# Attention scores of single heads as 32-row products, with unpadded keys and four larger buffers

## The chip, the cores and the metric

The kernel runs on one core of a Trainium2 chip. The metric is device time in microseconds (us), the median of the runs; lower is better. The profile is that of one execution, and its times count from the start of its span.

## The reference, cut to what matters

The input x is 8 batches of 512 tokens by 128 features. A macaron layer is computed in 32-bit floats:

```
x = x + 0.5 * moe(layernorm(x))       # 8 experts, hidden 512, all are applied and summed
x = x + attention(layernorm(x))       # 16 heads of 8 dimensions, causal
x = x + 0.5 * moe(layernorm(x))

moe:       acc += (silu(x @ wg[e]) * (x @ wu[e])) @ wd[e]   for the 8 experts
attention: q, k = rotary(q), rotary(k);  q = q / sqrt(8)
           scores = q @ k.T + q @ rel[clip(j - i, -32, 32)].T    (causal)
           attn = softmax(scores);  ctx = attn @ v + attn @ rel[...];  out = ctx @ wo.T
```

## The kernel before

**The expert passes.** A pass applies all eight experts to one batch. There are 16 passes (8 before the attention, called A, and 8 behind it, called B), each with 32 units of 128 hidden features. A unit is nine products on TensorE, each of 128 stationary columns and 512 moving ones: three for gate (L794, L795, L798), three for up (L730 to L732), two for down and one for down_lo (L813, L814, L821). Three products stand for one, because each operand is split in a high and a low part in the format fp32r. Between them ScalarE makes tanh (L942) and the high part hid_hi (L948), VectorE two products (L1073, L1079) and GpSimd the low part hid_lo (L1247). HB counts the buffers of hid, HH those of hid_hi and hid_lo.

**The attention.** It runs among the units of the passes, batch by batch. The 16 heads of a batch are worked in four groups of four (HG groups, the four places of a group are HQ). There are 32 groups in all (8 batches by 4). A group has four query tiles i = 0 to 3 of 128 queries, and tile i sees the first 128 (i + 1) keys. Its scores are made in 11 tasks, since a bank of PSUM holds 512 columns: one task of four heads for i = 0 (4 x 128 columns), two of two heads for i = 1 (2 x 256), four of one head for i = 2 (384 columns) and four of one head for i = 3 (512 columns). Each task is one product at L876.

A head has 8 dimensions, and q and k have two parts each, so the four part-by-part products of a head take 32 rows of the array. In the tile qq the rows of the four heads of a group are interleaved, every fourth row belonging to one head. The keys lie in k_pad, [128, 2, 4, 512]: for each of the four places a copy in which only that head's 32 rows hold keys and the other 96 rows are zeros. A product over all 128 rows so gives one head's scores. Eight memsets on GpSimd set the zeros once (step `zero`, L1276). q and k go through DRAM to get there: `qk_store` writes each of them with two DMAs of 512 KB, so that each part lies there twice; `load_q` reads 256 KB on ScalarE's queue, `load_k` reads four times 64 KB on SP's queue.

After the scores VectorE adds the relative windows (near, L1176), finds the extreme value (largest, L1181) and, for the tasks called lent (all but the first two of a group), shifts it (L1187). ScalarE takes the exponentials (L993): of lent tasks into exps (EB buffers, which frees the bank of PSUM), of the others in place. It rounds them (L1004, L1006), and GpSimd (L1262, lent tasks) or VectorE (L1194) makes the low part. PB counts the buffers of probs, TB those of the turned probabilities probs_t. SP stores and transposes them by DMA. `values` (L894) multiplies them with v on TensorE, in products of 25 stationary columns that go to 32 columns of the array each, four of them side by side. Then come the relative part of the values (L903), the scaling and the output projection (L912). L866 is q by the relative embeddings, L742, L736 and L834 are transposes.

**The order.** A planner in the kernel's Python lays all steps out in time. Each step has an engine, a cost, a due time (moved by the table `LATER`), and steps that it follows. At each turn the step that can start first is taken, among those of an engine the one that is due first. This gives each engine's instruction order, and which of the six shared banks of PSUM (`work`) a step takes. Real waits are by semaphores. Some costs that it uses (us):

```
if name in ("gate", "up", "down", "down_lo", "project") and (start > clock["PE"] or after_short):
    takes += 0.1                                    # after_short: the last was scores of i < 2
step("PE", 0.02 + columns / 2286, due[k], "scores", k, ..., done_with(back(k, 2)))
step("PE", 0.25 + 0.106 * sum(i + 1 for i in tiles), ..., "values", ...)
```

Of the kernel before, what the change touches and what calls it, by code (L numbers as in the profile page):

```python
# [8 lines left out]
def macaron_kernel(nc, x_d, wg_d, wu_d, wd_d, watt_d, wo_d, rel_g_d, rel_g0_d, rel_c_d, rel_c0_d,  # L9
# [9 lines left out]
    P = 128  # L19
# [16 lines left out]
    HB = 4  # L36
    HH = 3
# [3 lines left out]
    TB = 8  # L41
    PB = 4
    EB = 2
# [36 lines left out]

    def lent(k):

        return k % GK in (2, 3, 4, 5, 6, 7, 8, 9, 10)
# [12 lines left out]
    def quad_of(k):  # L96
# [11 lines left out]
    LATER = {"acc": -978.2, "attention_sum": -208.7, "band_turn": -699.6, "band_values": -929.8, "constants":  # L108
             1096.3, "denominators": 28.6, "down": 37.0, "down_lo": -142.5, "exp": -242.6, "fill": 586.2, "gate": 24.5,
             "gated": 194.7, "hi": -68.2, "largest": -205.0, "ln_hi": -593.7, "ln_lo": -686.7, "ln_rstd": 997.7,  # L110
             "ln_scaled": 0.6, "ln_stats": -1428.5, "ln_turned": -206.6, "lo": -358.6, "load_band": -996.6, "load_expert":
             -534.8, "load_k": 240.4, "load_q": -776.5, "load_window": 15.1, "load_x": -477.7, "near": -174.1, "outproj":
             -259.7, "p_hi": -298.3, "p_lent": -422.1, "p_lo": -1717.7, "p_turn": 143.5, "prepare_hi": -276.9,
             "prepare_lo": -63.6, "product": 18.1, "project": -160.8, "project_v": 49.6, "qk_hi": -1103.2, "qk_lo": -870.7,
             "qk_store": -526.1, "qrel": 26.2, "qrel_copy": -311.3, "qrel_store": -969.6, "recip": -772.7, "rotate":
             1048.0, "scale": -1250.2, "scores": -114.7, "shift": -653.9, "split_hi": 221.4, "split_lo": -79.7, "spread":
             -435.5, "store": 442.5, "store_band": -318.1, "sum": 728.2, "sum_turned": -570.0, "tanh": -286.1, "up": 27.3,
             "v_add": 384.8, "v_split": 128.2, "values": -612.1, "zero": 1356.1}

    def step(engine, takes, time, name, arg, *after, lands=None, ordered=()):  # L120
        before = []
        if name in ("p_lo", "p_lent", "shift"):
# [47 lines left out]
    for i in range(8):  # L170
        step("POOL", 0.9, 50, "zero", i, ("gate", 10 + 2 * i))
# [37 lines left out]
    for p, (kind, t) in enumerate(PASSES):  # L209
# [22 lines left out]
        for i in range(2):  # L232
# [3 lines left out]
            step("SP", 1.3, at, "qk_store", (t, i), ("qk_lo", (t, i)),  # L236
                 (("load_q", "load_k")[i], HG * (t + 1 - VB) - 1 if t >= VB else None), lands=4.5)

    for t in range(B):
        for g in range(HG):  # L240
# [33 lines left out]
        for k in range(NK * t, NK * (t + 1)):  # L274
            g, i, a = TASKS[k % NK]
            quad, columns = quad_of(k), HEADS[i] * (i + 1) * P
            step("PE", 0.02 + columns / 2286, due[k], "scores", k, ("load_q", quad // NT),
                 ("load_k", quad // NT), done_with(back(k, 2)))
            step("DVE", 0.07 + HEADS[i] * (P if i == 0 else W) / (960 if i < 2 else 580), due[k] + 0.5, "near", k, ("scores", k),
# [53 lines left out]
    while len(order) < len(steps):  # L333
# [17 lines left out]
        if engine == "PE":  # L351
            after_short = name == "scores" and TASKS[arg % NK][1] < 2
# [30 lines left out]
    q_h = nc.dram_tensor("q_scratch", [VB * 4 * P * L], F32, kind="Internal")  # L383
    k_h = nc.dram_tensor("k_scratch", [VB * 4 * P * L], F32, kind="Internal")
# [3 lines left out]
    with ctx:  # L388
# [29 lines left out]
        k_pad = sb("k_pad", [P, 2, HQ, L], F32R)  # L418
# [17 lines left out]
        lanes = sb("lanes", [P, 2])  # L436
# [70 lines left out]
        s_zero = sem("k_pad_zeroed")  # L507
# [92 lines left out]
        def _(sp):  # L600
# [20 lines left out]
            for name, arg in order:  # L621
# [18 lines left out]
                if name == "qk_store":  # L640
# [3 lines left out]
                    if t >= VB:  # L644

                        sp.wait_ge((s_qld, s_kld)[i][1], (16, 64)[i] * (HG // 2) * (t + 1 - VB))
# [50 lines left out]
                if name == "load_k":  # L697
                    t, g = arg // HG, arg % HG
                    sp.wait_ge(s_qst[1], 32 * (t + 1))
                    if arg < 2:  # L700
                        sp.wait_ge(s_zero, 8)
                    else:
                        sp.wait_ge(s_sc, GK * (arg - 1))
# [639 lines left out]
```

## Time and profile before

| what | us |
|---|---|
| median of 3 runs (1336.12 to 1340.96) | 1336.65 |
| the profiled execution, its own time | 1328.16 |
| its span | 1326.4 |
| TensorE busy by the page | 1307.4 (99%) |
| VectorE busy | 1212.7 (91%) |
| ScalarE busy | 1062.8 (80%) |
| GpSimd busy | 1061.4 (80%) |

The duration that a record of a product gives includes the way through the array, and those of successive products overlap: a product of 512 columns shows as 0.39 us. So the busy share of TensorE says little, and what one product occupies is read from start to start. Weight loads (PEld) have records of their own; as a rule one runs while the product before it streams.

### The profile page before, as it was taken

How to read it: one execution, taken by the hardware profiler on the slowest of the kernel's cores; microseconds unless marked ns; L12 is line 12 of the kernel's file. 1: busy time of each engine (PE TensorE's matmuls, PEld its weight loads, DVE VectorE, ACT ScalarE, POOL GpSimd, SP SyncE). 2: the span in 40 equal slices, each digit the busy share in tenths (PEclk: the TensorE clock that was granted, in tenths of full speed). 3: DMA queues.
4: the chain of work that ended last, by engine and by line, in shares of the span. 5: the costliest groups of instructions: out<-in, count | busy, mean ns of one | idle time of the engine just before them, and what ended most of it. 6: DMA issues, size and time to landing. Idle time of an engine off the chain costs nothing. (4 is left out here: it accounts for less than half of the span.)

```text
span 1326.4 us, 28468 instructions
## 1 busy us (share of the span) xinstructions
PE 1307.4 (99%) x8334; PEld 1051.4 (79%) x8334; DVE 1212.7 (91%) x2611; ACT 1062.8 (80%) x2099; POOL 1061.4 (80%) x979
## 2 busy tenths in 40 slices
PE   8999999999999999999999999999999999999998
PEld 6888888787778787778888778887888778888787
DVE  6887999999999999999999999999999999998665
ACT  6866888878888888888888888887888888887565
POOL 7976888879878887797787878788778887878565
PEclk9999999999999999999999999999999999999999
DMA  6503899999999999999999999999999999997100
GB/s 190 163 1 118 160 217 228 201 224 229 215 222 215 199 197 194 243 196 202 200 209 208 216 206 200 197 227 205 198 206 198 206 219 206 204 188 138 23 5 8
DMA packets 718555, 241.39 MB, mean 182 GB/s; under 512 B 652480, under 2 KB 681920, under 8 KB 718400
## 3 DMA queue, kind: packets, MB, share of 16 engines
q1 hardware_dynamic: 562240, 180.84, 68.0%
q10 hardware_dynamic: 156160, 58.74, 22.4%
q8 instruction: 66, 1.08, 0.3%
q14 instruction: 89, 0.73, 0.2%
HBM read 77.33 MB, written 69.86 MB: 111 GB/s over the span
## 5 line engine op out<-in xcount | busy, mean ns | idle before, releaser
L1247 POOL TENSOR_TENSOR hid_lo<-hid,hid_hi 128x512 fp32r<-128x512 f32 x511 | 658.8, 1297 | 174.2 <-ACT hid_hi L948 92.7
L942 ACT ACTIVATE hid<-work 128x512 f32<-128x512 f32 x512 | 306.2, 600 | 100.9 <-PE work L798 72.0
L948 ACT CAST hid_hi<-hid 128x512 fp32r<-128x512 f32 x512 | 316.2, 625 | 88.2 <-PE acc L814 55.4
L1073 DVE SCALAR_TENSOR_TENSOR hid<-hid,work 128x512 f32<-128x512 f32 x512 | 343.9, 679 | 44.3 <-ACT hid L942 43.7
L1079 DVE TENSOR_TENSOR hid<-hid,work 128x512 f32<-128x512 f32 x512 | 346.3, 680 | 23.8 <-PE work L732 20.5
L1262 POOL TENSOR_TENSOR probs<-exps,probs 128x512 f16<-128x512 f32 (+1 forms) x288 | 304.1, 1061 | 62.0 <-ACT probs L1004 58.9
L1181 DVE TENSOR_REDUCE negmax<-work 128x1 f32<-128x384 f32 (+3 forms) x352 | 219.5, 632 | 0.5
L993 ACT ACTIVATE exps<-work,negmax_shifted 128x512 f32<-128x512 f32 (+2 forms) x320 | 187.6, 601 | 37.6 <-DVE negmax_shifted L1187 27.1
L821 PE MATMUL acc<-hid_lo,wd 128*128 128x512 f32 x512 | 207.2, 409 | 1.2 <-POOL hid_lo L1247 1.1
L730 PE MATMUL work<-xt,wu 128*128 128x512 f32 x512 | 205.1, 401 | 3.0 <-DVE rope L1163 1.3
L813 PE MATMUL acc<-hid_hi,wd 128*128 128x512 f32 x512 | 203.0, 396 | 1.5 <-ACT xn L959 0.7
L794 PE MATMUL work<-xt,wg 128*128 128x512 f32 x512 | 203.1, 397 | 1.4 <-ACT xt L935 0.8
L732 PE MATMUL work<-xt,wu 128*128 128x512 f32 x512 | 200.6, 392 | 0.0
L798 PE MATMUL work<-xt,wg 128*128 128x512 f32 x512 | 200.4, 392 | 0.0
L731 PE MATMUL work<-xt,wu 128*128 128x512 f32 x512 | 200.4, 391 | 0.0
L795 PE MATMUL work<-xt,wg 128*128 128x512 f32 x512 | 200.4, 391 | 0.0
L814 PE MATMUL acc<-hid_hi,wd 128*128 128x512 f32 x512 | 200.0, 391 | 0.0
L1004 ACT ACTIVATE probs<-exps 128x512 f16<-128x512 f32 (+1 forms) x288 | 167.4, 585 | 12.2 <-issue 4.7
L1176 DVE TENSOR_TENSOR work<-work,rel_win 128x160 f32<-128x160 f32 (+2 forms) x352 | 162.6, 470 | 10.7 <-PE work L876 8.6
L876 PE MATMUL work<-k_pad,qq 128*128 128x512 f32 (+1 forms) x352 | 130.5, 384 | 0.8 <-ACT exps L993 0.5
L730 PEld LDWEIGHTS work<-xt,wu 128*128 128x128 f32 x512 | 96.4, 188 | 28.8 <-DVE hid L1079 2.9
L813 PEld LDWEIGHTS acc<-hid_hi,wd 128*128 128x128 f32 x512 | 96.2, 188 | 23.8 <-ACT hid_hi L948 2.7
(100 smaller groups left out, 1735.0 us busy)
## 6 DMA issues: line engine op xcount, KB each, us to landing
rel_win<-rel_window_scratch ACTq DMA_DIRECT2D x128, 320.0 KB, 3.8
prob_window_scratch<-probs SPq DMA_DIRECT2D x384, 80.0 KB, 3.2
q_scratch<-rope SPq DMA_DIRECT2D x16, 512.0 KB, 4.0
qq<-q_scratch ACTq DMA_DIRECT2D x32, 256.0 KB, 3.6
k_scratch<-rope SPq DMA_DIRECT2D x16, 512.0 KB, 4.8
rel_window_scratch<-g_s SPq DMA_DIRECT2D x32, 256.0 KB, 3.3
k_pad<-k_scratch SPq DMA_DIRECT2D x128, 64.0 KB, 3.5
prob_window_scratch<-probs SPq DMA_DIRECT2D x32, 256.0 KB, 4.0
```

The costliest lines, as they stand in the source:

```text
L730: pe.matmul(out, w_hi, m_hi, start=start, stop=False)
L732: return pe.matmul(out, w_lo, m_hi, start=False, stop=stop)
L794: pe.matmul(bank[:, :], wg[:, HI, e, cols], x_hi, start=True, stop=False)
L813: pe.matmul(acc[:, :], wd[:, HI, e, cols], hid_hi[:, arg % HH, :], start=(k == 0), stop=False)
L821: pe.matmul(acc[:, :], wd[:, HI, e, cols], hid_lo[:, arg % HH, :], start=False, stop=(k == CH - 1)).then_inc(s_dlo, 1)
L942: act.activation(hid[:, arg % HB, :], work[bank_of["gate", arg]][:, :], ACT.Tanh, scale=0.5).then_inc(s_tanh, 1)
L948: act.copy(hid_hi[:, arg % HH, :], hid[:, arg % HB, :]).then_inc(s_hhi, 1)
L1073: dve.scalar_tensor_tensor(out=hid[:, arg % HB, :], in0=hid[:, arg % HB, :], scalar=1.0, in1=work[bank_of["gate", arg]][:, :], op0=ALU.add ...
L1079: dve.tensor_tensor(hid[:, arg % HB, :], hid[:, arg % HB, :], work[bank_of["up", arg]][:, :], ALU.mult).then_inc(s_hid, 1)
L1181: dve.tensor_reduce(negmax[:, place:place + len(places)], heads, AX.X, ALU.min).then_inc(s_max, 1)
L1247: pool.tensor_tensor(hid_lo[:, arg % HH, :], hid[:, arg % HB, :], hid_hi[:, arg % HH, :].bitcast(F32), ALU.subtract).then_inc(s_hlo, 1)
L1262: pool.tensor_tensor(probs[:, arg % PB, cols:2 * cols], exp_of(arg)[:, 0:cols], probs[:, arg % PB, 0:cols], ALU.subtract).then_inc(s_plent, 1)
```

## The change

- **Rows by heads.** The weights are laid out so that each head of a group has 32 rows of its own, side by side, in qq and in the new tile kk, [128, 2, 512]. k_pad and its memsets go.
- **Scores.** For i = 1 to 3 a product takes only the 32 rows of one head (`rows = slice(R * places[0], ...)`), stationary 32 x 128 and moving 32 x (128 (i + 1)). Tasks are issued in pairs: `leads(k)` names the first task of a pair, and both are due at the same time. The two have different rows of the array and different banks. A task of i = 1 has two heads in one bank, so it needs two products: both tasks' first heads, then a wait until these are complete (s_first), then the two others (the new step `second`).
- **i = 0** stays one product over all 128 rows for four heads, by a small padded tile k_apart, [128, 4, 128], which GpSimd makes for each group (kk times a 0/1 mask; the new step `k_apart`, 32 times).
- **Stores and loads.** q is stored with two DMAs of 256 KB, k with one of 512 KB; load_q reads each row twice into neighbouring partitions (256 KB as before), load_k is two DMAs of 128 KB.
- **Buffers.** HB 4 to 5, HH 3 to 4, TB 8 to 9, EB 2 to 3; scores may run ahead of the exponentials by 4 tasks (AHEAD) instead of 2.
- **The planner** has new costs for the steps and a new LATER table, so the order of the steps on all engines is another.

```diff
-    HB = 4
-    HH = 3
+    HB = 5
+    HH = 4
-    TB = 8
+    TB = 9
+    AHEAD = 4
-    EB = 2
+    EB = 3
...
+    def leads(k):
+        return k - (k % GK - 1) % 2 if k % GK else k
...
-    for i in range(8):
-        step("POOL", 0.9, 50, "zero", i, ("gate", 10 + 2 * i))
...
-            step("SP", 1.8, first - 14, "load_k", gg, ("qk_store", (t, 1)), ("zero", 7),
+            step("SP", 1.1, first - 14, "load_k", gg, ("qk_store", (t, 1)),
                  ("scores", GK * (gg - 1) - 1 if gg >= 2 else None), lands=LATE + 1)
+            step("POOL", 1.2, first - 6, "k_apart", gg, ("load_k", gg), ("scores", GK * (gg - 1) if gg else None))
...
-            step("PE", 0.02 + columns / 2286, due[k], "scores", k, ("load_q", quad // NT),
-                 ("load_k", quad // NT), done_with(back(k, 2)))
+            reach = (i + 1) * P
+            head = leads(k)
+            step("PE", 0.02 if head != k else 0.1 + (columns if i == 0 else reach) / 2286, due[head], "scores", k,
+                 ("load_q", quad // NT), ("k_apart" if i == 0 else "load_k", quad // NT), done_with(back(k, AHEAD)),
+                 ordered=[("second", k - 1)] if k % GK == 3 else [])
+            if i == 1:
+                step("PE", 0.02 if head != k else 0.1 + reach / 2286, due[head], "second", k, ("scores", k),
+                     ordered=[("scores", head + 1)] if head == k else [])
...
-            after_short = name == "scores" and TASKS[arg % NK][1] < 2
+            after_short = name in ("scores", "second") and TASKS[arg % NK][1] < 2
...
-        k_pad = sb("k_pad", [P, 2, HQ, L], F32R)
+        kk = sb("kk", [P, 2, L], F32R)
+        k_apart = sb("k_apart", [P, HQ, P], F32R)
...
-                    for copy in range(2):
-                        sp.dma_start(bass.AP((q_t, k_t)[i], base + copy * (1 + i) * P * L,
-                                             [[L, P], [(2 - i) * P * L, 2], [1, L]]),
-                                     rope[:, :, :]).then_inc(s_qst[i], 16)
+                    if i == 0:
+                        for part in (HI, LO):
+                            sp.dma_start(bass.AP(q_t, base + part * HG * L, [[2 * HG * L, R], [L, HG], [1, L]]),
+                                         rope[:, part, :]).then_inc(s_qst[0], 16)
+                    else:
+                        sp.dma_start(bass.AP(k_t, base, [[L, P], [P * L, 2], [1, L]]), rope[:, :, :]).then_inc(s_qst[1], 16)
...
-                    for a in range(HQ):
-                        sp.dma_start(k_pad[a:P:HQ, arg % 2, a, :].bitcast(F32),
+                    for part in (HI, LO):
+                        sp.dma_start(kk[part:P:2, arg % 2, :].bitcast(F32),
...
                 if name == "scores":
                     bank = take_bank(name, arg)
                     if arg % GK == 0:
                         pe.wait_ge(s_qld[gg % 2], 16 * (gg // 2 + 1))
-                        pe.wait_ge(s_kld[gg % 2], 64 * (gg // 2 + 1))
-                    pe.matmul(bank[:, 0:len(places) * keys], qq[:, gg % 2, i * P:(i + 1) * P],
-                              k_pad[:, gg % 2, places[0]:places[-1] + 1, 0:keys],
-                              start=True, stop=True).then_inc(s_sc, 1)
+                        pe.wait_ge(s_ka, gg + 1)
+                        pe.matmul(bank[:, 0:HQ * P], q_tile, k_apart[:, :, :], start=True, stop=True).then_inc(s_sc, 1)
+                    else:
+                        if arg % GK == 1:
+                            pe.wait_ge(s_kld[gg % 2], 32 * (gg // 2 + 1))
+                        rows = slice(R * places[0], R * (places[0] + 1))
+                        pe.matmul(bank[:, 0:keys], q_tile[rows, :], kk[rows, gg % 2, 0:keys],
+                                  start=True, stop=True).then_inc(s_first if i == 1 else s_sc, 1)
+                if name == "second":
+                    bank = work[bank_of["scores", arg]]
+                    if leads(arg) == arg:
+                        pe.wait_ge(s_first, 2 * (gg + 1))
+                    rows = slice(R * places[1], R * (places[1] + 1))
+                    pe.matmul(bank[:, keys:2 * keys], q_tile[rows, :], kk[rows, gg % 2, 0:keys],
+                              start=True, stop=True, skip_group_check=True).then_inc(s_sc, 1)
...
-                if name == "zero":
-                    pool.memset(k_pad[:, arg // 4, arg % 4, :].bitcast(F32), 0.0).then_inc(s_zero, 1)
+                if name == "k_apart":
+                    pool.wait_ge(s_kld[arg % 2], 32 * (arg // 2 + 1))
+                    if arg:
+                        pool.wait_ge(s_sc, GK * (arg - 1) + 1)
+                    else:
+                        pool.wait_ge(s_const, 16 * 12)
+                    pool.tensor_tensor(k_apart[:, :, :],
+                                       kk[:, arg % 2, None, 0:P].bitcast(F32).to_broadcast([P, HQ, P]),
+                                       lanes[:, 2:2 + HQ, None].to_broadcast([P, HQ, P]), ALU.mult).then_inc(s_ka, 1)
...
     def dh_major(w):
-        return np.asarray(w).reshape(H, DH, P).transpose(1, 0, 2)
+        return np.asarray(w).reshape(HQ, H // HQ, DH, P).transpose(0, 2, 1, 3)
```

## Rows read from the trace of the kernel before

**Rows 1.** The page: busy time of each engine, and the span in 40 slices.
```profile
PE 1307.4 (99%) x8334; PEld 1051.4 (79%) x8334; DVE 1212.7 (91%) x2611; ACT 1062.8 (80%) x2099; POOL 1061.4 (80%) x979
PEclk9999999999999999999999999999999999999999
DMA  6503899999999999999999999999999999997100
```

**Rows 2.** Timeline of TensorE's products: start, duration, what.
```profile
600.88 1.05 PE L912 MATMUL work<-wo,ctx_s 128*128 128x128 f32 x8
...
620.52 0.39 PE L795 MATMUL work<-xt,wg 128*128 128x512 f32 x1
620.75 0.39 PE L798 MATMUL work<-xt,wg 128*128 128x512 f32 x1
620.98 0.39 PE L821 MATMUL acc<-hid_lo,wd 128*128 128x512 f32 x1
621.20 0.51 PE L876 MATMUL work<-k_pad,qq 128*128 128x384 f32 x2
621.55 0.40 PE L730 MATMUL work<-xt,wu 128*128 128x512 f32 x1
```

**Rows 3.** Groups of products by line and form: busy us, mean ns.
```profile
L731 PE MATMUL work<-xt,wu 128*128 128x512 f32 x512 | 200.4, 391 | 0.0
L876 PE MATMUL work<-k_pad,qq 128*128 128x512 f32 x224 | 88.7, 407 | 0.6 <-ACT exps L993 0.5
L876 PE MATMUL work<-k_pad,qq 128*128 128x384 f32 x128 | 41.8, 343 | 0.1
L894 PE MATMUL ctx_p<-probs_t,values 128*25 128x128 f16 x2560 | 47.4, 220 | 0.4 <-DMA probs_t<-probs 0.4
L912 PE MATMUL work<-wo,ctx_s 128*128 128x128 f32 x256 | 34.0, 276 | 0.4 <-ACT exps L993 0.3
L894 PEld LDWEIGHTS ctx_p<-probs_t,values 128*25 128x25 bf16 x2560 | 36.2, 94 | 23.4 <-issue 23.4
```

**Rows 4.** Busy time by stretch, columns PE, PEld, DVE, ACT, POOL, clock, DMA share, GB/s.
```profile
0.00:20.00 20.00, 15.13 (x57) 11.79 (x58) 10.87 (x28) 12.27 (x23) 11.29 (x16) 0.91 0.70 216
400.00:1200.00 800.00, 793.05 (x5405) 637.36 (x5407) 765.76 (x1692) 673.25 (x1352) 652.65 (x600) 1.00 1.06 206
```

**Rows 5.** Timeline of products and weight loads around one `values` step.
```profile
610.18 0.39 PE L732 MATMUL work<-xt,wu 128*128 128x512 f32 x1
610.49 0.68 PEld L894 LDWEIGHTS ctx_p<-probs_t,values 128*25 128x25 bf16 x48 [0.35 <-issue]
610.50 0.85 PE L894 MATMUL ctx_p<-probs_t,values 128*25 128x128 f16 x48
611.28 0.19 PEld L876 LDWEIGHTS work<-k_pad,qq 128*128 128x128 f32 x1
611.28 0.50 PE L876 MATMUL work<-k_pad,qq 128*128 128x512 f32 x1
611.38 0.19 PEld L730 LDWEIGHTS work<-xt,wu 128*128 128x128 f32 x1
611.61 0.39 PE L730 MATMUL work<-xt,wu 128*128 128x512 f32 x1
```

**Rows 6.** Timeline of products and weight loads where a load came late.
```profile
449.04 0.19 PEld L730 LDWEIGHTS work<-xt,wu 128*128 128x128 f32 x1
449.14 0.19 PEld L731 LDWEIGHTS work<-xt,wu 128*128 128x128 f32 x1
449.06 0.48 PE L730 MATMUL work<-xt,wu 128*128 128x512 f32 x1
449.37 0.39 PE L731 MATMUL work<-xt,wu 128*128 128x512 f32 x1
```

**Rows 7.** GpSimd's groups, and who waited for the scores.
```profile
L1262 POOL TENSOR_TENSOR probs<-exps,probs 128x512 f16<-128x512 f32 x160 | 186.4, 1170 | 39.5 <-ACT probs L1004 37.5 <-PE acc L821 2.0
L1276 POOL MEMSET k_pad<- 128x512 f32 x8 | 4.1, 526 | 0.0
DVE work L1176 <- PE work L876: 8.6, 23, 1.0
```
**Rows 8.** DMA in all, and issues: what, count, KB each, us to landing.
```profile
DMA packets 718555, 241.39 MB, mean 182 GB/s; under 512 B 652480, under 2 KB 681920, under 8 KB 718400
...
q_scratch<-rope SPq DMA_DIRECT2D x16, 512.0 KB, 4.0
k_scratch<-rope SPq DMA_DIRECT2D x16, 512.0 KB, 4.8
k_pad<-k_scratch SPq DMA_DIRECT2D x128, 64.0 KB, 3.5
```

More of the change, by code:

```diff
@@ L104, in macaron_kernel @@
     LANDS = {"PE": 0.35, "ACT": 0.35, "DVE": 0.35, "POOL": 0.35, "SP": 2.6}
[L108 to L118, printed above, removed]
@@ new lines, in macaron_kernel @@
+    LATER = {"acc": -943.7, "attention_sum": -408.4, "band_turn": -235.6, "band_values": -957.6, "constants":
+             1078.1, "denominators": 18.0, "down": 52.4, "down_lo": 38.2, "exp": -351.9, "fill": 545.0, "gate": 26.4,
+             "gated": 104.8, "hi": 81.4, "k_apart": -747.6, "largest": -28.6, "ln_hi": -738.4, "ln_lo": -1126.1, "ln_rstd":
+             1224.7, "ln_scaled": 285.5, "ln_stats": -1507.3, "ln_turned": -10.2, "lo": -464.1, "load_band": -1193.4,
+             "load_expert": 202.6, "load_k": -36.6, "load_q": -1025.4, "load_window": 650.5, "load_x": -482.1, "near":
+             -39.9, "outproj": -136.5, "p_hi": -477.1, "p_lent": -748.7, "p_lo": -1658.0, "p_turn": 436.6, "prepare_hi":
+             370.9, "prepare_lo": -508.5, "product": 65.6, "project": -351.7, "project_v": 67.8, "qk_hi": -1234.1, "qk_lo":
+             -867.0, "qk_store": -84.9, "qrel": -333.1, "qrel_copy": -92.6, "qrel_store": -692.4, "recip": -1022.1,
+             "rotate": 1128.9, "scale": -1248.1, "scores": 42.2, "second": -175.7, "shift": -651.7, "split_hi": -323.3,
+             "split_lo": 111.2, "spread": -550.9, "store": 87.3, "store_band": -479.8, "sum": 295.4, "sum_turned": -39.8,
+             "tanh": -608.3, "up": 29.4, "v_add": 115.9, "v_split": -101.5, "values": 46.1}
@@ L120, in step @@
     def step(engine, takes, time, name, arg, *after, lands=None, ordered=()):
         before = []
-        if name in ("p_lo", "p_lent", "shift"):
+        if name in ("p_lo", "p_lent", "shift", "second"):
             before = [(name, arg - by) for by in range(1, GK + 1)]
@@ L276, in macaron_kernel @@
             quad, columns = quad_of(k), HEADS[i] * (i + 1) * P
-            step("PE", 0.02 + columns / 2286, due[k], "scores", k, ("load_q", quad // NT),
-                 ("load_k", quad // NT), done_with(back(k, 2)))
-            step("DVE", 0.07 + HEADS[i] * (P if i == 0 else W) / (960 if i < 2 else 580), due[k] + 0.5, "near", k, ("scores", k),
+            reach = (i + 1) * P
[6 more added lines that the diff above has]
+                     ordered=[("scores", head + 1)] if head == k else [])
+            step("DVE", 0.07 + HEADS[i] * (P if i == 0 else W) / (960 if i < 2 else 580), due[k] + 0.5, "near", k, ("second" if i == 1 else "scores", k),
                  ("load_window", quad))
@@ L351, in macaron_kernel @@
         if engine == "PE":
-            after_short = name == "scores" and TASKS[arg % NK][1] < 2
+            after_short = name in ("scores", "second")
         open_steps[engine].remove((time, key))
@@ L435, in macaron_kernel @@
         ident = sb("ident", [P, P])
-        lanes = sb("lanes", [P, 2])
+        lanes = sb("lanes", [P, 2 + HQ])
         stats = sb("stats", [P, NT, 6])
@@ L868, in _ @@
                     done.then_inc(s_g, 1)
-                if name == "scores":
+                if name in ("scores", "second"):
                     quad, i, places, keys = task(arg)
                     gg = quad // NT
+                    q_tile = qq[:, gg % 2, i * P:(i + 1) * P]
+                if name == "scores":
                     bank = take_bank(name, arg)
@@ L1321 @@
     window = np.repeat(np.where(w > i + R, 1e30, 0.0), HQ, axis=1)
-    lanes = np.repeat([[0.0, 1.0], [1.0, -1.0], [0.0, 1.0], [1.0, -1.0]], DH * HQ, axis=0)
+    lanes = np.tile([[0.0, 1.0], [1.0, -1.0], [0.0, 1.0], [1.0, -1.0]], (DH * HQ, 1))
+    lanes = np.concatenate([lanes, np.repeat(np.eye(HQ), R, axis=0)], axis=1)
     arrays = {
```

40 lines of the change are left out of this document (20 added, 20 removed).

## The prediction

> **What bounds the kernel now.** I read the page first. TensorE is busy 99% of the span, VectorE 91%, ScalarE and GpSimd 80% [rows 1], and the granted clock is full but for the start [rows 1, 4]. A product's record overlaps the next one's, so I took the timeline for what a product occupies. Products of 512 columns start 0.227 us apart, two of 384 take 0.35 together (0.175 each), and eight of 128 end after 1.05, so (1.05 - 0.28) / 7 = 0.11 each [rows 2]. With the counts [rows 1, 3]: 16 passes x 32 units x 9 = 4608 expert products at 0.227 are 1046 us; scores 224 x 0.227 + 128 x 0.175 = 73; `values` 56 (below); the output projection 256 x 0.11 = 28; the other 558 of 8334 (160 wide, 398 narrow) 80. The sum is 1283 of a span of 1326. Of the 43 left, 5 are idle time in the first 20 us [rows 4] and some 5 more lie at the start and the end; about 30 are short waits in the run. So TensorE sets the time almost alone: what it saves or loses is seen in full, and only these 30 us can absorb or give anything. Behind it comes VectorE: from 400 to 1200 us it is busy 765.8 of 800, 95.7% [rows 4].
>
> **The gain: two heads at a time.** Per group of heads the tasks of i = 1 to 3 cost 2 x 0.227 + 4 x 0.175 + 4 x 0.227 = 2.06 us now [rows 2, 3]. If the two products of a pair stream side by side, i = 2 costs 2 x 0.175, i = 3 2 x 0.227, and i = 1 two rounds of 256 columns, 0.227: together 1.03. That saves 1.03 a group, 33 us over 32 groups. That products stream side by side is shown for the four column strips of `values`: 48 products of 128 columns take 0.85, where one after the other they would take over 5 [rows 2, 5]. For row strips no row shows it.
>
> **The price: cutting the array and joining it.** The expert products use the whole array, and each pair of scores stands among them. The trace has one step of this kind, `values`, which cuts the array in column strips. I read it edge by edge [rows 5]. In: the product before starts at 610.18 and has streamed by 610.41, but the first weight load starts at 610.49, so 0.09 is lost; ordinary loads run while the product before streams. Out: the block ends at 611.35 and a product of it lasts 0.22 [rows 3], so the last starts at 611.13 and its 128 columns have streamed by 611.19. The next load starts at 611.28, 0.09 later, and its product streams only when the load after it starts, at 611.38: a load of 128 columns, unhidden, is 0.10. So an excursion of `values` costs 0.09 + 0.20 = 0.3. (Its 12 rounds of four take (611.13 - 610.50) / 11 = 0.057; 64 blocks of 10 rounds on average make 64 x 0.87 = 56 us.) Its first load has 25 columns and shows next to nothing; that of a score product has 128 and would add 0.10 if nothing hides it. Another late load costs the same: the next product starts 0.31 after it instead of 0.227 [rows 6].
>
> Pairs are five a group (one of i = 1, two each of i = 2 and 3). In the pair of i = 1 the second round waits until both first products are complete. A product of 512 columns lasts 0.39 [rows 2] and streams 0.227, so 0.17 passes before the wait can end, and a load of 0.10 follows: 0.27. If expert products are put between the rounds, it is a sixth excursion instead, at 0.3 to 0.4. Per excursion x the balance of a group is 5x + 0.27 - 1.03; it is even at x = 0.15. By rows:
> - x = 0 (nothing is lost at the edges, as between scores and expert products today [rows 2]): -0.76 a group, -24 us; without the second round's wait either, -33.
> - x = 0.1 for each of six excursions (one unhidden load [rows 6], also what the planner's new entry says): -0.43, -14.
> - x = 0.3 (`values` as it stands): +0.74, +24.
> - x = 0.4 (with the load of 128 columns): +1.24, +40.
>
> The bounds are -33 and +40. I take 0.35 to 0.4: `values` is the only row in which the array is cut and joined, and both its edges lose time that no wait on another engine explains (its idle time is put down to "issue", 23.4 us over 64 blocks [rows 3]). That gives +32 to +40.
>
> The Trainium skill speaks against this change too: TensorEngine Tiling (Array Packing), Tiling Modes, says that changing the tiling mode, other than going from tile to tile, drains TensorE. The 0.09 at both edges of `values` agrees with it; for row strips no run here shows it yet. By this rule the sum would be the +24 to +40 above, without it the -24.
>
> **The buffers.** HH, HB and EB give ScalarE and GpSimd room: both are at 80%, and what they and VectorE wait for is mostly TensorE. AHEAD lets scores run two more tasks ahead, TB one more task before its `values`. TensorE's share of their delays lies within the 30 us of short waits, so this is the upper bound of the gain, 0 the lower one (none of the 30 need be theirs; a loss only by a worse order, below). I take 8, a quarter. If TensorE grows slower, the others are late less often: I take another 8 off as absorbed. The cover for that is VectorE's 4.3% of free time, 34 us per 800 [rows 4].
>
> **Work on other engines and queues.** GpSimd loses eight memsets of 0.53 and gets 32 masks of 128 x 512, nearest row 1.17 [rows 7]: +37 us, to 83%. It is hidden as long as `lo` is not late; a group has some 33 us (1050 / 32), and this is 1.2 of them, of GpSimd's 20% idle. Without cover it would be 37 us; I count 0, since the mask only needs the keys and the scores before the last, and is due early. Behind it on GpSimd's queue stand `lo` and p_lent, at most 1.2 late. DMA: the stores of q and k go from 16.8 to 8.4 MB of 241 and the loads of keys from four issues to two [rows 8]: 3% less, at latencies that nothing on TensorE waits for. I count 0, with -3 as bound. VectorE's near, largest and shift keep their shapes; near of i = 1 waits for the second round, some 0.3 later, and scores are seldom what VectorE waits for (8.6 us in 23 waits [rows 7]): 0.
>
> **Sum.** 40 - 8 - 8 = +24, against the profiled execution's 1328.2 (span 1326.4): 1352. The median lies 8.5 us above that execution, so 1361 for the median, 1.8% slower.
>
> **Rivals.**
> 1. *The array is cut by rows without loss, or with one unhidden load.* Then x is 0 to 0.1, and the gain of streaming side by side stays: -14 to -24, and 8 from the buffers, -22 to -32: about 1310 (1305 to 1318). For it: scores among expert products cost nothing extra today, and a row strip keeps all 128 output columns where `values` changes them. Against it: both edges of `values`. It decides at 0.15 us per excursion. The Trainium skill, TensorE: Matmul & The Clock Gate, Part 3, says that loads for other row groups, or for the background weight buffer, are pulled ahead of running products. By that rule the time would be this rival's; the load of `values` that starts only after the stream disagrees, for columns. Within this rival VectorE is the floor: 95.7% of 800 us leaves at most 34 us per 800, so it allows the gain but without slack. Chance 0.33.
> 2. *Half price.* x is near 0.2: 5 x 0.2 + 0.27 - 1.03 = +0.24, +8 us, and the buffers give 8: 1337, no change. For it: a drained array of 32 rows might empty faster than the 0.09 of `values`. Chance 0.13.
> 3. *No streaming side by side.* The gain of 33 is absent, the edges cost as forecast: +33 more, 1385 to 1390. Against it: `values` streams side by side. Chance 0.04.
> 4. *The forecast*, 1343 to 1377: chance 0.50.
>
> **How the numbers follow.** 1361 is the forecast's own sum; its own range is 1343 to 1377, from x = 0.3 with all of the buffers' 16 (1345) to x = 0.4 with nothing absorbed (1377). The other large case stands at 1305 to 1318, so a range for 8 in 10 has to reach into it: 1308 to 1374. It leaves out rival 3 and the outer edges of rival 1 and of the forecast, together about 0.15. A measurement of this kernel can tell about 0.5%, 6.7 us. Faster holds rival 1 (0.33); same is most of rival 2 (0.13); slower is the forecast, rival 3 and nothing else (0.54).
>
> **What would show it.** In the timeline around a pair: the load of the first score product should start about 0.09 after the expert product before it has streamed, both products of a pair should start within 0.01 of each other, and the expert product behind them should stream 0.2 after the pair's last column. From the start of the expert product before a pair of i = 3 to that of the one behind, forecast 0.227 + 0.4 + 0.227 = 0.85, rival 1 0.45 to 0.55. The granted clock should stay full. Idle time before the loads of the scores line should appear as "issue", some 5 times 32 with 0.1 or more each. GpSimd's busy time should grow by 35 us. The prediction is wrong if loads of the pair run during the product before, or if TensorE's short waits fall by much more than 16 us.

## The result, and the profile after

The changed kernel takes 1390.5 us (median of 4 runs, 1388.7 to 1392.7) against 1336.4 in the same comparison: 54 us slower, ratio 1.041 with an interval of 1.036 to 1.046. The forecast was 1361, with a range of 1308 to 1374. The sign was right; the forecast's size, +24, was a little under half of what came.

The page after, beside that of [rows 1]: busy time of each engine, and the slices with TensorE's clock.

```profile
span 1390.8 us, 28607 instructions
...
PE 1371.2 (99%) x8398; PEld 1029.7 (74%) x8398; DVE 1222.9 (88%) x2611; ACT 1055.1 (76%) x2099; POOL 1087.8 (78%) x1003
...
PEclk9999999999999999999999999999999999999999
```

TensorE is still busy 99%, the busy shares of the other engines fell by 2 to 4 points, and the clock stays full. So the 64 us that the span grew by lie in what TensorE has to do. (GpSimd's busy time grew by 26 us, where the forecast expected 35.) TensorE's busy time can't say where its time goes, since records overlap; the timeline can. Here are the products, then the weight loads, around one pair of i = 3 of the changed kernel.

```profile
601.32 0.39 PE L743 MATMUL work<-xt,wu 128*128 128x512 f32 x1
601.55 0.39 PE L744 MATMUL work<-xt,wu 128*128 128x512 f32 x1
601.87 0.50 PE L895 MATMUL work<-kk,qq 32*128 32x512 f32 x2
602.30 0.50 PE L806 MATMUL work<-xt,wg 128*128 128x512 f32 x1
602.63 0.40 PE L807 MATMUL work<-xt,wg 128*128 128x512 f32 x1
```

```profile
601.33 0.19 PEld L744 LDWEIGHTS work<-xt,wu 128*128 128x128 f32 x1
601.87 0.18 PEld L895 LDWEIGHTS work<-kk,qq 32*128 32x128 f32 x2 [0.35 <-issue]
602.30 0.19 PEld L806 LDWEIGHTS work<-xt,wg 128*128 128x128 f32 x1 [0.25 <-issue]
602.41 0.19 PEld L807 LDWEIGHTS work<-xt,wg 128*128 128x128 f32 x1
```

The two products of the pair are one row of 0.50, so they stream side by side. The last whole product starts at 601.55 and has streamed by 601.78; the pair's loads start at 601.87, 0.09 later, and are not hidden. The pair streams from about 601.98 to 602.20, the next load starts at 602.30, and its product streams when the load after it starts, at 602.41. From 601.55 to 602.41 is 0.86, forecast was 0.85. Less the two streams of 0.227 an excursion (one cutting of the array into rows and its joining again) costs 0.40: the highest value in the forecast's list. It is some 0.09 + 0.11 going in and 0.09 + 0.11 coming out.

What the forecast did not have is in the next rows, the same kernel at one of its tiles i = 1.

```profile
608.66 0.39 PE L744 MATMUL work<-xt,wu 128*128 128x512 f32 x1
608.98 0.38 PE L895 MATMUL work<-kk,qq 32*128 32x256 f32 x1
609.29 0.50 PE L825 MATMUL acc<-hid_hi,wd 128*128 128x512 f32 x1
609.63 0.40 PE L826 MATMUL acc<-hid_hi,wd 128*128 128x512 f32 x1
609.95 0.38 PE L895 MATMUL work<-kk,qq 32*128 32x256 f32 x1
610.39 0.38 PE L903 MATMUL work<-kk,qq 32*128 32x256 f32 x1
610.70 0.50 PE L825 MATMUL acc<-hid_hi,wd 128*128 128x512 f32 x1
611.03 0.40 PE L826 MATMUL acc<-hid_hi,wd 128*128 128x512 f32 x1
611.27 0.56 PE L878 MATMUL work<-rel_g,qq 128*128 128x128 f32 x4
611.76 0.38 PE L903 MATMUL work<-kk,qq 32*128 32x256 f32 x1
```

The four products of this i = 1 make three excursions and none streams beside another: expert products and the query-by-embedding products stand between them in TensorE's order. `due[head]` gives both tasks of a pair the same due time, but the second is a step of its own; when no bank is free for it yet, the planner can take another step. This is one of the worst cases; in others both products of a round do go together. I counted runs of 32-row products over all of TensorE's records:

```
excursions into 32-row products, changed kernel                 229   (7.2 a group; 160 pairs were meant as 5 a group)
  two products of 512 columns, of 384, of 256                    54, 45, 45
  one product alone: of 512, of 384, of 256                      20, 37, 18
  two rounds of an i = 1 with a wait between them                  9
  three products                                                   1
```

By tasks, 73 of the 229 belong to i = 1, where 32 were meant; i = 2 has 82 and i = 3 has 74, where 64 each were meant. So more than half of the 69 surplus ones come from i = 1, most of all because other products stand between its two rounds.

The waits of the weight loads show the drained edges as "issue", as forecast, 166 + 31 times before score products and some 140 times behind them.

```profile
PEld work L895 <- issue: 58.0, 166, 0.4
...
PEld work L806 <- issue: 12.7, 58, 0.2
PEld work L903 <- issue: 11.5, 31, 0.7
...
PEld acc L833 <- issue: 8.4, 37, 0.2
PEld acc L825 <- issue: 6.1, 31, 0.2
```

Priced from the records, from the start of the product before an excursion to the stream of the one behind, less that product's 0.227: 0.63 for a pair of 512 columns, 0.57 of 384, 0.52 of 256, and the same for a single one. Over the 229 that is 134 us, where the tasks of i = 1 to 3 took 66 before (the forecast's 2.06 a group): +68. The spans of the two profiles differ by 64 (1390.8 - 1326.4).

### The profile page after: what moved, and what is told of

Its sections match the earlier page's. It is cut to its first block, busy times and chain, and to the rows that moved or that the text cites. A ratio compares the mean times of both kernels' runs of the same rounds, so it can differ in the third digit from the quotient of the medians.

```text
span 1390.8 us, 28607 instructions
## 1 busy us (share of the span) xinstructions
PE 1371.2 (99%) x8398; PEld 1029.7 (74%) x8398; DVE 1222.9 (88%) x2611; ACT 1055.1 (76%) x2099; POOL 1087.8 (78%) x1003
## 4 chain that ended last, share of the span: by engine, by line
PE 94%; DMA 2%; issue 1%; DVE 1%; ACT 1%; POOL 1%; POOLq 0%; ACTq 0%; SPq 0%; DVEq 0%
PE work L806 10%; PE work L742 9%; PE acc L825 9%; PE acc L833 9%; PE work L744 9%; PE work L743 9%; PE work L810 8%; PE work L807 8%; PE acc L826 8%; PE work L895 5%; PE ctx_p L920 3%; PE work L938 2%; DMA probs_t<-probs 1%; PE ctx_p L929 1%; PE work L903 1%
## 5 line engine op out<-in xcount | busy, mean ns | idle before, releaser
L974 ACT CAST hid_hi<-hid 128x512 fp32r<-128x512 f32 x512 | 312.3, 625 | 49.1 <-PE acc L826 26.1
L806 PE MATMUL work<-xt,wg 128*128 128x512 f32 x512 | 213.9, 418 | 1.4 <-ACT xt L961 0.8
L1207 DVE TENSOR_REDUCE negmax<-work 128x1 f32<-128x384 f32 (+3 forms) x352 | 211.2, 633 | 0.3
L825 PE MATMUL acc<-hid_hi,wd 128*128 128x512 f32 x512 | 210.2, 411 | 0.1
L1019 ACT ACTIVATE exps<-work,negmax_shifted 128x512 f32<-128x512 f32 (+2 forms) x320 | 183.7, 603 | 32.1 <-DVE negmax_shifted L1213 26.8
L810 PE MATMUL work<-xt,wg 128*128 128x512 f32 x512 | 201.4, 393 | 0.0
L807 PE MATMUL work<-xt,wg 128*128 128x512 f32 x512 | 201.2, 393 | 0.0
L826 PE MATMUL acc<-hid_hi,wd 128*128 128x512 f32 x512 | 200.3, 391 | 0.0
L1202 DVE TENSOR_TENSOR work<-work,rel_win 128x160 f32<-128x160 f32 (+2 forms) x352 | 155.9, 475 | 43.0 <-PE work L895 27.8
L806 PEld LDWEIGHTS work<-xt,wg 128*128 128x128 f32 x512 | 96.5, 188 | 34.4 <-issue 12.7
```

The source lines that it names most:

```text
L806: pe.matmul(bank[:, :], wg[:, HI, e, cols], x_hi, start=True, stop=False)
L807: pe.matmul(bank[:, :], wg[:, LO, e, cols], x_hi, start=False, stop=False)
L810: pe.matmul(bank[:, :], wg[:, HI, e, cols], x_lo, start=False, stop=True).then_inc(s_gate, 1)
L825: pe.matmul(acc[:, :], wd[:, HI, e, cols], hid_hi[:, arg % HH, :], start=(k == 0), stop=False)
L974: act.copy(hid_hi[:, arg % HH, :], hid[:, arg % HB, :]).then_inc(s_hhi, 1)
```

## Experiments

The kernels from here on, but for two that run TensorE alone, move the probabilities and the bands by plain DMAs of the same bytes instead of turned ones and take the reciprocals of a constant, so their attention is not the reference's. The base and the changed kernel were run in this form too. The first four rows of the table were run in one set, c3 to c6 in a second, c7 and c8 in a third. The kernel before, run beside them, took 1331.8, 1335.4 and 1333.5 us in the three sets, so a difference of up to 4 us between kernels of different sets is not clear of noise.

| run | what | us (lowest to highest) |
|---|---|---|
| base_with_copies | kernel before | 1318.6 (1318.1 to 1319.5) |
| changed_with_copies | changed kernel | 1385.9 (1384.9 to 1387.1) |
| c1_all_rows | changed, scores over all rows | 1325.3 (1323.6 to 1326.5) |
| c2_pairs_together | changed, pairs never split | 1368.1 (1367.3 to 1368.4) |
| c3_one_product | c1, i = 1 as one product a task | 1322.1 (1321.3 to 1324.6) |
| c4_no_masks | c3 without GpSimd's masks | 1320.6 (1319.6 to 1322.0) |
| c5_one_cut | base, 32 single excursions | 1330.0 (1328.0 to 1332.0) |
| c6_ten_cut | base, 297 excursions | 1428.5 (1428.3 to 1428.6) |
| c7_four_heads | changed, four heads at once | 1726.1 (1725.2 to 1727.4) |
| c8_old_buffers | c3 with the old buffer counts | 1347.4 (1347.0 to 1350.5) |

### The price by itself: strips_own

In short, one block (16 of each case, of seven cases):

```diff
+ for _ in range(16):
+     four whole products
+     pe.matmul(strip0, w[0:32, 0:P], m[0:32, 0:512])     # the first case: one strip of 32 rows
```

> A kernel of its own, none of the reference's work: only TensorE is busy, with seven stretches of 16 blocks. A block is four whole products (128 rows, 128 stationary and 512 moving columns, fp32r) and then one of seven cases. Read from start to start of whole products. Theory (the edges of the cut cost 0.40 whatever stands beside them): one strip of 32 rows 0.40 + 0.227 over a block without it; two strips and four strips the same, since they stream side by side; one strip of 64 rows and two the same 0.63; the same strip of 32 rows twice 0.85; a product of 32 stationary columns 0.53 (its load is short). Rival (the price belongs to the attention kernel's waits): a strip alone costs 0.227 more and four side by side too. Second rival (strips don't stream side by side): four cost 1.3.

```profile
84.45 0.19 PEld L53 LDWEIGHTS strip<-m,w 32*128 32x128 f32 x4 [0.37 <-issue]
84.45 0.50 PE L53 MATMUL strip<-m,w 32*128 32x512 f32 x4
84.88 0.77 PEld L49 LDWEIGHTS full<-m,w 128*128 128x128 f32 x4 [0.24 <-issue]
84.88 1.20 PE L49 MATMUL full<-m,w 128*128 128x512 f32 x4
```

These are loads and products of this kernel at four strips: again there is one row of 0.50 for all four, and idle time on both sides put down to "issue", though no other engine has anything to do. From the whole product before the case to the second one behind it, less the 0.454 of two whole products, the medians of 16 blocks are:

```
one strip of 32 rows            0.64     one strip of 64 rows       0.63
two strips of 32 rows           0.64     two strips of 64 rows      0.64
four strips of 32 rows          0.64     32 fp32r columns           0.24
the same strip of 32 rows twice 0.86
```

So an excursion is 0.227 of stream and 0.41 of edges, for one strip or four. As nothing else runs in this kernel, it is a cost of TensorE itself. The last case missed: a product of 32 stationary columns in fp32r, expected at 0.53, costs no edge at all.

### The two bases

```diff
-                    sp.dma_start_transpose(turned_probs(arg)[:, 0:blocks, :],
-                                           probs[:, arg % PB, 0:blocks * P]).then_inc(turned(arg)[0], 16)
+                    sp.dma_start(turned_probs(arg)[:, 0:blocks, :],
+                                 probs[:, arg % PB, 0:blocks * P].rearrange("p (b q) -> p b q", q=P)
+                                 ).then_inc(turned(arg)[0], 16)
```

> The kernel before, but the probabilities (352 DMAs) and the bands (32) are moved by plain DMAs of the same bytes instead of turned ones, and the reciprocals are taken of constants: so the attention's values are not the reference's, all sizes and waits stay. It is the base for the runs that follow. If TensorE alone sets the time, as both traces say, it stays at 1336 (1326 to 1340). If the turned DMAs or their landing set it, it falls by more than 15.

> The changed kernel with the same plain copies and reciprocals of constants as the base. Theory (TensorE's edges): the difference of the two kernels, 54, stays within 6, so about 1390. Rival (the DMA queues take part in the loss): it falls under 40.

Both missed. The base is 13 us faster than the kernel before in the same set (ratio 0.989, 0.987 to 0.992), so turned DMAs cost the kernel before something after all. (The constant reciprocals were not tried by themselves.) The waits of TensorE and its loads for other engines and DMAs, added up from the profiles (a wait of both counts twice), fall from 50 to 32 us, and TensorE's idle time (span less busy) from 19.0 to 13.2. In the kernel before, the turned probabilities and one wait for the turned bands read:

```profile
probs_t<-probs SPq DMA_TRANSPOSE x352, 4.0
...
PEld ctx_p L903 <- DMA band_t<-bands: 3.0, 3, 1.5
```

In the base there is no such wait, and the plain ones land sooner:

```profile
probs_t<-probs SPq DMA_DIRECT2D x224, 256.0 KB, 3.3
probs_t<-probs SPq DMA_DIRECT2D x128, 192.0 KB, 2.9
```

The larger part of the waits that fall is for ScalarE and VectorE; how the DMAs reach those was not followed. The changed kernel gains only 5 (1390.5 to 1385.9, of different sets), and the difference grows from 54 to 67, about the +68 read from the records.

### Whole rows, or pairs kept together

c1_all_rows:

```diff
-                        rows = slice(R * places[0], R * (places[0] + 1))
+                        rows = slice(0, P)
```

> The changed kernel with plain copies, and each score product of i = 1 to 3 takes all 128 rows instead of its head's 32 (so it sums four heads; order, stores, loads, waits and buffers stay). The trace of the changed kernel has 229 excursions into 32-row products, each costs 0.40. Theory (the edges of the cut are what costs): minus 229 x 0.40 = 92, plus 25 because paired products now stream one after another, so 67 less than the changed kernel with plain copies, about 1324 (1318 to 1334), at or under the base. Rival (the new order, the stores and GpSimd's masks are at fault): it stays over 1360, since those are all kept. Second rival (half each): 1345 to 1355.

c2_pairs_together, in the planner's choice of TensorE's next step:

```diff
+                if engine == "PE" and kept and key != kept[0]:
+                    continue
...
+                if key[0] == "scores" and leads(key[1]) == key[1] and key[1] % GK:
+                    partner = ("scores", key[1] + 1)
+                    if missing[partner] > 1:
+                        continue
+                    start = max([start, held[1]] + [given[what] for what in steps[partner][4]])
```

> The changed kernel with plain copies, but the planner lets a pair start only when both banks are free and puts nothing between its products (for i = 1 the two second products too): 160 excursions in TensorE's order instead of 229. Theory (the split pairs are what the forecast missed): 69 x 0.40 = 28 less, 8 less for streaming side by side, 7 more for 23 further waits between the rounds of i = 1, so 29 under the changed kernel with plain copies, about 1361 (1354 to 1368), which is also what was forecast for the change. Rival (holding two banks at a time costs as much as the splits): 1380 to 1395.

With whole rows the changed order, its loads, masks and buffers take 1325.3: 60.6 of the 67.3 us are gone by an edit that removes the cut alone, and with it the streaming side by side. The expectation was 67. The rival that holds the order responsible for the loss is out; the other 6.7 us stay with what c1 keeps. Of c1, the page and the waits of weight loads:

```profile
PE 1304.1 (99%) x8398; PEld 1057.7 (80%) x8398; DVE 1209.5 (92%) x2611; ACT 1050.5 (79%) x2099; POOL 1087.4 (82%) x1003
```

```profile
PEld ctx_p L921 <- issue: 22.0, 64, 0.4
PEld ctx_p L930 <- issue: 8.4, 32, 0.3
...
PEld work L904 <- PE work L896: 3.3, 9, 0.4
```

The "issue" rows of score products and of the products behind them are gone; that of `values` stands, 22 us in 64 blocks, as before the change. Between the rounds of i = 1, waits of 3.3 us are left.

Pairs kept together take 1368.1: 17.8 less, not 29. The records show 160 excursions as meant, and the price of each kind as before, but the four products of i = 1 now take 0.98 from edge to edge: 0.40 of edges, two streams of 0.11 and 0.36 between them, where the forecast had 0.27. It had 0.17 from the stream's end to the product's end and 0.10 for the load, and nothing for the 0.09 (median of 32) between the record's end and the load of the second round. From its page and the waits of its weight loads:

```profile
span 1366.6 us, 28607 instructions
...
PE 1343.5 (98%) x8398; PEld 1025.3 (75%) x8398; DVE 1218.4 (89%) x2611; ACT 1053.1 (77%) x2099; POOL 1087.3 (80%) x1003
...
PEld work L912 <- issue: 41.4, 119, 0.4
...
PEld work L920 <- PE work L912: 9.2, 32, 0.3
PEld acc L850 <- issue: 6.2, 28, 0.2
PEld work L912 <- ACT exps L1036: 5.8, 16, 0.4
```

The 32 waits between rounds are all there. By the same prices the excursions fall from 134 to 108 us, 8 more than the time fell. TensorE is idle for 23.1 us of this span, where changed_with_copies has 15.7, and the loads' wait for exponentials is 5.8, where that one has 2.9. So waiting for two free banks seems to take most of the 8; it was not tried by itself. Even in this form, as the change was meant, it is 49.5 us slower than the base.

### What the rest of the change does: c3, c4 and c8

c3 restores one product for a task of i = 1, c4 also drops the masks, c8 takes c3 with the old counts (the five constants are drawn into one line here):

```diff
+                        pe.matmul(bank[:, 0:len(places) * keys], q_tile,
+                                  kk[:, gg % 2, None, 0:keys].to_broadcast([P, len(places), keys]), ...)   # c3
...
-                    pool.tensor_tensor(k_apart[:, :, :], ...)                                        # c4
...
-    HB, HH, TB, EB, AHEAD = 5, 4, 9, 3, 4
+    HB, HH, TB, EB, AHEAD = 4, 3, 8, 2, 2                                                             # c8
```

> As c1_all_rows (1325.3), but a task of i = 1 is one product of 2 x 256 columns again, without second rounds and their wait: TensorE then does the same scores products as the kernel before. Theory (second rounds cost what c1 has over the base): the trace of c1 has 3.3 us in 9 such waits and 1 us for shorter products, so 1321 (1318 to 1323). Rival (order or masks): stays at 1325.

> As c3_one_product, and GpSimd makes no masks: the product of i = 0 takes the keys directly, four times (all heads summed). 32 operations of some 1.2 us are gone from GpSimd. Theory (hidden, as forecast): the same as c3 within 2. Rival (they delay hid_lo): 4 to 8 less than c3.

> As c3_one_product (1322), but HB, HH, TB, EB and AHEAD are 4, 3, 8, 2 and 2 as before. If the buffers gave the 8 us that the forecast took: 1330. If they gave nothing, as the idle times of both traces suggest: 1320 to 1325.

c3 is 3.3 us under c1 (1325.3 to 1322.1), as much as the wait of the second rounds in c1's rows, though the two are of different sets. The masks make no difference that shows (1322.1 to 1320.6, and the runs overlap); GpSimd's record of one is 1.05 us, hidden as forecast. What is left, 1320.6 against the base's 1318.6, has the new order, buffers, stores and loads: together they show no gain. c8 went beyond both expectations: with the old counts the new due times are 25 us worse than with the new ones, 29 worse than the old order with the same counts. So counts and due times belong together, and this run can't say what a buffer is worth with the old due times. In the trace TensorE's loads wait for VectorE's products and GpSimd's hid_lo:

```profile
PEld work L743 <- DVE hid L1098: 9.5, 27, 1.3
PEld acc L834 <- POOL hid_lo L1266: 7.7, 14, 1.1
PEld work L807 <- DVE hid L1092: 6.9, 17, 1.3
```

### Is any of it absorbed: c5 and c6

```diff
-                    pe.matmul(bank[:, 0:len(places) * keys], qq[:, gg % 2, i * P:(i + 1) * P],
-                              k_pad[:, gg % 2, places[0]:places[-1] + 1, 0:keys],
+                    rows = slice(0, R) if arg % GK == 5 else slice(0, P)        # c6: if arg % GK
+                    pe.matmul(bank[:, 0:len(places) * keys], qq[rows, gg % 2, i * P:(i + 1) * P],
+                              k_pad[rows, gg % 2, places[0]:places[-1] + 1, 0:keys],
```

> The base with plain copies (1318.6), but one task in eleven (the third of the four of i = 2) takes 32 rows instead of 128, so its scores lack three quarters of the rows: 32 excursions are added and nothing else. Theory (nothing is absorbed): 32 x 0.41 = 13, so 1332 (1329 to 1334). Rival (the short waits absorb the first few, as the forecast assumed): 1319 to 1325.

> The base with plain copies, but all ten tasks of i = 1 to 3 take 32 rows (the other rows are left out), one after another, in the old order: 297 excursions, none with products side by side. Theory: 297 x 0.41 less some 11 that share an edge with values (0.1 to 0.2 each) = 120, so 1438 (1430 to 1446). Rival (engines behind TensorE catch up, so each further excursion costs less): 1405 to 1425.

c5 adds 11.4 us for 32 excursions, 0.36 each, of an edge price of 0.39 in its records (a product of 384 columns, 0.687 from start to start, + 0.107 for the late load behind - 0.227 - 0.175). c6 adds 109.9 for 297, 0.37 each; its records sum to 116. So 5 to 9% is absorbed, in the first excursions as in all of them; the base was run in another set, and 1 us more or less in c5 moves its 9% by as much again. c5 lies within its expectation. c6 lies 1.5 us under its range and 3.5 over the range of its rival, but an excursion costs as much there as in c5, so further ones do not get cheaper.

### Four heads at once: c7

The measured prices say where a cut could pay: one excursion for four heads costs 0.63 at 512 columns, where four whole products cost 0.91. c7 does this for i = 2 and 3, leaves i = 1 whole, and counts 0.4 for an excursion in the planner.

```diff
-        return k - (k % GK - 1) % 2 if k % GK else k
+        return k - (k % GK - 3) % 4 if k % GK >= 3 else k
...
+                if key[0] == "scores" and key[1] % GK in (3, 7):      # start with four banks free, nothing between
```

> The changed kernel with plain copies, but a task of i = 1 is one product over all rows (it sums four heads), and for i = 2 and i = 3 all four heads go at once, 32 rows and a bank each: the planner starts them only when four of the six banks are free. Two excursions a group, 64 in all. By the measured prices i = 2 costs 0.40 + 0.175 instead of 0.70, i = 3 0.40 + 0.227 instead of 0.91: 0.40 a group, 13 us less than c3_one_product (1322). Theory (TensorE's time decides): 1309 (1304 to 1314), under the base of 1318.6. Rival (four banks held at a time starve gate and up, and VectorE gets its work in lumps): 1322 or more.

The rival was right, and far beyond its number: 1726. The records show 64 excursions. Where they stand among whole products (13 of the 64, medians) they cost what was computed (0.70 and 0.76 from start to start, where a single strip has 0.69 and 0.75); but TensorE is idle for 16% of the span. Two stretches of its windows (busy time of PE, PEld, DVE, ACT, POOL; clock, DMA) and two rows of its waits:

```profile
300.00:500.00 200.00, 156.10 (x958) 112.49 (x957) 142.47 (x315) 121.64 (x243) 114.74 (x111) 0.78 0.62 174
...
1300.00:1500.00 200.00, 131.11 (x1010) 93.64 (x1010) 138.06 (x317) 124.14 (x254) 112.69 (x106) 0.70 0.76 212
```

```profile
PE ctx_p L933 <- DMA probs_t<-probs: 79.5, 28, 8.0
...
PE work L916 <- ACT exps L1032: 21.7, 16, 2.8
```

The likely reason is that the planner seldom finds four of six banks free, so the scores come late and in lumps; in the trace TensorE then waits for exponentials and for the probabilities' DMAs. In the two stretches TensorE is busy 156 and 131 of 200 us, and the granted clock is 0.78 and 0.70 on average, so for part of the time it is at 1.2 GHz. What the lower clock costs was not separated. An order made for lumps was not tried, so whether four at once can pay stays open.

### More strips: strips_more

> TensorE alone again, blocks of four whole products and then one case. Theory (each change between the whole array and strips costs 0.41 at its two edges, whatever the strip): the last 32 rows 0.64 more than a block without it; 64 stationary columns of all rows 0.23 (no cut, as 32 columns in strips_own); 32 rows and then 64 rows 0.41 + 2 x 0.227 + a further edge of 0.20; four strips of 384 columns 0.58. Column strips in bf16: one at the first place 0.23, one at the second place or four at once about 0.23 + 0.3. Rival (drained only at the first and last of a place): no difference between the two column places.

By the same measure as in strips_own: the last 32 rows 0.64; 64 fp32r columns 0.24; four strips of 384 columns 0.58; a strip of 32 rows and then one of 64 1.07. The latter is two streams and 0.61, three edges of 0.20: going from strips of one size to another costs an edge as well. Column strips in bf16 cost 0.53 to 0.54, at the first place, at the second, and four at once: 0.30 of edges. The first of these missed the expectation of 0.23. They differ from the whole products around them in format as well, and so do the products of `values`; what part of the 0.30 is the change of format was not tried.

## Why the prediction came out as it did

**Right.** *The bound.* TensorE sets nearly all of the time; the busy shares of the other engines fell. *The gain.* Products of one pair stream side by side, and four do so too; rival 3 is out. That its 1385 to 1390 lie nearest to the measured time is chance (and 1361 + 33 would be 1394). *The price of an excursion.* x = 0.40, read from `values` plus an unhidden load of 128 columns, was measured in the kernel (0.40) and alone (0.41). Of the bounds from 0 to 0.4 the upper one holds, so rivals 1 and 2 are out. The Trainium skill, TensorEngine Tiling (Array Packing), Tiling Modes, says that a change of mode drains TensorE. The rows of row strips agree: the 0.09 before each load, and the third edge between strips of 32 and of 64 rows. The fp32r products of 32 and 64 stationary columns show no edge (0.24); whether they change the mode no run here tells. *The work on other engines.* Masks make no difference that shows (c3 and c4).

**Wrong, first: the number of excursions.** The step "pairs are five a group (one of i = 1, two each of i = 2 and 3)" took the name of the change for TensorE's order. It was 7.2 a group. c2 measures what the splits cost: 17.8 us, net of the waits that they spare. The forecast had a sixth excursion for i = 1 only as a variant and added nothing for it, and it had none for i = 2 and 3, although each pair has to find two of six banks.

**Wrong, second: the sum took 16 us off for which no experiment shows a gain.** "I take 8, a quarter" for the buffers: with the cut removed and plain copies, order, buffers and loads show no gain (c4 is 2 us over the base). "Another 8 off as absorbed": c5 and c6 show that 5 to 9% of added TensorE time is absorbed, 2 to 4 us of 40. The short waits were real, but few of them vanish when TensorE gets longer.

**Smaller.** The wait between rounds is 0.36 instead of 0.27: +3 us. Without the two deductions the forecast's own upper sum was +40; with 3 for the rounds and 2 for the remaining parts (c4) it stands at 45, and the change with its pairs kept measures 49.5 (c2 against the base). The 4.5 between them are not assigned; TensorE's idle time is 10 us longer in c2 than in the base. Added up: the forecast's 24, 16 for the deductions, 18 for the splits, 5 for the smaller parts and these 4.5 make the 67 of the pair with plain copies.

The bridge between 67 and 54 stays open in part. Plain copies take 13 us off the kernel before and 5 off the changed one. With turned DMAs the waits of TensorE and its loads, added up as above, go from 50 us before to 45 after; with plain copies they go from 32 to 37. So the real change did remove some late deliveries: the changed kernel's trace has no wait of TensorE for turned probabilities or bands. Whether the ninth buffer of turned probabilities, another buffer or TensorE's slower pace does it was not tried. The scatter plays in too: the kernel before took 1329 to 1341 us, and its profiled execution, 1328, is 8 us under its median. So in the real pair some 8 to 13 us of the edges' 67 were given back, and there the forecast's buffer term, or its absorbed one, may have had its place.

## What to carry to other kernels

Before cutting the array for small products, price the two edges (0.40 us here, as much as 1.8 whole products of 512 columns) against what streams side by side: a pair gains 0.23 and loses, and three would gain 0.05 by these prices, an estimate. Four gain 0.28, if they really go together and the wait for their banks costs less than that, which c7 did not reach. Count excursions in the order of instructions, not in the tasks: two steps with the same due time are only neighbours if something keeps them so. And what a planner's cost table says of an operation that no trace has shown yet (0.1 here) is a guess; the nearest row of another operation (0.3 for `values`) was three times closer to the measured 0.40.

## What the runs showed of the hardware

- Cutting the array by rows and joining it costs the same for one, two or four strips and for 32 or 64 rows (0.63 to 0.64 with its stream of 0.227). The weight loads at both edges start some 0.09 after the last column has streamed.
- Products of 32 or 64 stationary columns in fp32r that start at the first column cost no edge (0.24 in all), while one of 32 columns in bf16 at the same place, among fp32r products, costs 0.30 of edges. Whether the format or its change makes the difference was not tried.
- Two cuts of different kinds side by side don't share an edge in full: between strips of 32 and 64 rows 0.20 is lost again.
- Replacing turned DMAs by plain ones of the same bytes (landing after 2.9 to 3.3 us instead of 4.0), together with constant reciprocals, made a kernel whose TensorE is busy 99% faster by 13 us.
